# Two normalisations and the small operations of the softmax shifts on the Pool engine, and second scores one slot later over 128 rows

## What is computed

```python
x = x + tanh(g_xattn) * attention(layernorm(x), ctx, ctx, w_q, b_q, w_k, b_k, w_v, b_v, w_o, b_o)   # causal
x = x + tanh(g_ffn) * (mx_quantize(layernorm(x)) @ mx_quantize(weight).T + bias)
# layernorm(x) = (x - mean) / sqrt(var + 1e-5) over the width
# mx_quantize: blocks of 32 along the width, scale = max|block| / 7.5, then the nearest FP6 (E2M3) value
```

## Time and profile before

| what | value |
|---|---|
| median of 3 runs | 1609.66 us (1608.75 to 1612.53) |
| the profiled execution | 1625.08 us |
| its span | 1623.0 us |
| mean granted clock of PE in it | 0.955 of full speed |
| busy: PE, DVE, ACT, POOL | 89%, 76%, 65%, 36% of the span |

### The profile page before, as it was taken

The page is one execution under the profiler, slowest core; times in us unless marked ns, Lnnn a source line. Parts: engine busy times, 40 slices in busy tenths (PEclk is TensorE's granted clock), DMA queues, the critical chain, the costliest instruction groups (busy, mean ns, idle before and its releaser), DMA issues.

```text
span 1623.0 us, 34272 instructions
## 1 busy us (share of the span) xinstructions
PE 1448.8 (89%) x10333; PEld 1240.7 (76%) x10333; DVE 1233.2 (76%) x4731; ACT 1060.2 (65%) x3483; POOL 581.8 (36%) x881
## 2 busy tenths in 40 slices
PE   4788989999999998999998999999999999989976
PEld 4677777778878777877777878777787777778764
DVE  3677877878777788787787777777877778887863
ACT  2476667666666766766666666676666677766661
POOL 2223333443233343333333333344332344433343
PEclk9898999999999999999999999999999999999997
DMA  5244434343443443444444344344344344434420
GB/s 207 54 118 116 118 105 117 93 118 105 122 120 98 119 104 100 123 118 112 111 97 112 106 118 120 102 106 116 99 124 118 100 123 103 113 102 102 105 65 26
DMA packets 101807, 175.79 MB, mean 108 GB/s; under 512 B 14828, under 2 KB 18936, under 8 KB 101624
## 3 DMA queue, kind: packets, MB, share of 16 engines
q1 hardware_dynamic: 101624, 173.60, 41.3%
HBM read 56.11 MB, written 16.78 MB: 45 GB/s over the span
## 4 chain that ended last, share of the span: by engine, by line
DVE 42%; PE 29%; ACT 13%; issue 12%; DMA 2%; SPq 1%; POOL 0%; DVEq 0%; ACTq 0%
DVE all_probs L784 8%; PE proj L472 7%; DVE stack L820 7%; ACT all_probs L637 6%; PE proj L474 6%; PE proj L473 6%; DVE qk L841 4%; PE oT_ps L543 3%; DVE xs L897 3%; PE proj L565 3%; DVE stats L825 3%; DVE oT_lo L867 2%; DVE x L849 2%; DVE shift_rows L811 2%; DMA stack<-qk 2%
## 5 line engine op out<-in xcount | busy, mean ns | idle before, releaser
L637 ACT ACTIVATE all_probs<-all_probs,neg_max 128x128 f32<-128x128 f32 (+1 forms) x1024 | 457.8, 451 | 320.1 <-DVE neg_max L784 313.5
L784 DVE CUSTOM_DVE_ANT_0 all_probs<-s_ps,causal 128x128 f32<-128x128 f32 (+1 forms) x1024 | 322.4, 351 | 241.5 <-PE s_ps L515 226.3
L408 POOL TENSOR_SCALAR_AFFINE_SELECT all_probs<-all_probs 128x256 f32<-128x256 f32 x512 | 209.1, 409 | 777.4 <-ACT all_probs L656 777.4
L656 ACT ACTIVATE all_probs<-sT_ps 128x384 f32<-128x384 f32 x512 | 250.1, 489 | 139.3 <-PE sT_ps L528 138.1
L527 PE MATMUL sT_ps<-stack 104*128 104x256 f32 x512 | 178.0, 348 | 28.5 <-DVE stack L820 27.5
L637 ACT ACTIVATION_READ_ACCUMULATOR all_probs<-all_probs,neg_max 128x1 f32 x1024 | 196.3, 192 | 0.0
L472 PE MATMUL proj<-cT_hi,wk_hi 128*128 128x256 f32 x512 | 155.6, 304 | 29.0 <-DVE cT_lo L861 29.0
L514 PE MATMUL s_ps<-stack 96*128 96x256 f32 x512 | 155.7, 304 | 24.0 <-DMA stack<-qk 19.1
L820 DVE CAST stack<-shift_rows 8x256 fp32r<-8x256 f32 x512 | 159.5, 312 | 10.2 <-DVE shift_rows L811 0.6
L472 PE MATMUL proj<-aT_hi,wq_hi 128*128 128x256 f32 x512 | 152.2, 297 | 4.5 <-DVE aT_lo L861 4.5
L473 PE MATMUL proj<-cT_lo,wk_hi 128*128 128x256 f32 x512 | 146.2, 286 | 0.0
(11 more groups left out here) (133 smaller groups left out, 3918.2 us busy)
## 6 DMA issues: line engine op xcount, KB each, us to landing
stack<-qk SPq DMA_DIRECT2D x768, 128.0 KB, 2.4
cs<-in_ctx SPq DMA_DIRECT2D x32, 512.0 KB, 3.7
xs<-in_x SPq DMA_DIRECT2D x32, 512.0 KB, 4.5
x<-in_x SPq DMA_DIRECT2D x32, 512.0 KB, 3.9
out<-x SPq DMA_DIRECT2D x32, 512.0 KB, 3.1
vs<-in_L_xattn_w_k SPq DMA_DIRECT2D x2, 512.0 KB, 5.1
all_probs<-in_L_xattn_w_q SPq DMA_DIRECT2D x2, 512.0 KB, 6.4
all_probs<-in_L_xattn_w_v SPq DMA_DIRECT2D x2, 512.0 KB, 10.4
```

The costliest lines, as they stand in the source:

```text
L408: nc.gpsimd.affine_select(out=p, in_=p, compare_op=ALU.is_ge, fill=no, base=0, pattern=[[0, 2], [1, P]], channel_multiplier=-1).then_inc(t ...
L637: last = nc.scalar.activation(probs[:, n % P_RING, cols], probs[:, n % P_RING, cols], ACT.Exp, scale=-1.0, bias=neg_max[:, G % R_RING, t, ...
L656: nc.scalar.activation(probsT[:, n % PT_RING, :], sT_ps[n % 2][:, 0:3 * P], ACT.Exp, scale=-1.0).then_inc(pT_ok, 1)
L784: last = nc.vector.tensor_tensor_reduce(probs[:, n % P_RING, cols], s_ps[n % 2][:, cols], causal[:, (1 - t) * P:], 1.0, MASKED, ALU.add, A ...
```

## The change

- `shifts` is divided. POOL now computes ln(den) - neg_max twice (unrounded, and rounded as the high part), their difference `rest`, and near_one * den. DVE only adds near_one - 1 to `rest` as the low part, transposes and copies as before. The high part no longer holds the correction.
- `normalise` and `normalise_x` run on POOL: `normalise` one slot earlier in the program's order (2 slots behind `o`, ahead of `scaled`), `normalise_x` behind the power in slot 10, ahead of that slot's `shifts`.
- `T_LAG` is 7 and `AV_LAG` 16. With them values are weighed in slots 6 and 14 and split in 7 and 15, and `SLOT_PARTS` moves the light slots along.
- `stack` has 128 rows; rows 104 to 127 are set to zero at the start, and the second scores run over 128 rows.

```diff
-T_LAG = 6
-AV_LAG = 15
+T_LAG = 7
+AV_LAG = 16
-SLOT_PARTS = (3, 3, 3, 3, 3, 1, 3, 3, 3, 4, 3, 3, 3, 1, 4, 3)
+SLOT_PARTS = (3, 3, 3, 3, 3, 3, 1, 3, 3, 4, 3, 3, 3, 4, 1, 3)
...
-        stack = sb("stack", [ROWS + SHIFT, 2, 3 * PAIR, S], F32R)
+        stack = sb("stack", [P, 2, 3 * PAIR, S], F32R)
...
@@ gpsimd
+            nc.gpsimd.memset(stack[ROWS:, 1, :, :].bitcast(F32), 0.0).then_inc(zeros_ok, 1)
...
+            def shifts(G):
+                its = G % R_RING
+                pool.wait_ge(max_ok, GROUP * (G + 1))
+                pool.wait_ge(ln_ok, G + 1)
+                if G:
+                    pool.wait_ge(rows_ok, G)
+                nc.gpsimd.tensor_tensor(bare, ln_den[:, its], neg_max[:, its], ALU.subtract).then_inc(bare_ok, 1)
+                nc.gpsimd.tensor_tensor(shift_cols[:, :, 0:GROUP].bitcast(F32R), ln_den[:, its], neg_max[:, its],
+                                        ALU.subtract).then_inc(bare_ok, 1)
+                pool.wait_ge(bare_ok, 2 * G + 2)
+                nc.gpsimd.tensor_tensor(rest, bare, shift_cols[:, :, 0:GROUP], ALU.subtract).then_inc(r_ok, 1)
+                pool.wait_ge(exp_ok, G + 1)
+                nc.gpsimd.tensor_tensor(near_one[:, :, :], near_one[:, :, :], den[:, its], ALU.mult).then_inc(r_ok, 1)
+            def normalise(b, t):
+                pool.wait_ge(rs2, 2 * b + t + 1)
...
+                nc.gpsimd.tensor_scalar(yz[:, t, :], x1[:, b % 2, t, :], mom2[:, t, 0:1], var2[:, t:t + 1],
+                                        ALU.subtract, ALU.mult).then_inc(y_ok, 1)
+            def normalise_x(b):
+                pool.wait_ge(rs1, b + 1)
+                for t in range(T):
+                    nc.gpsimd.tensor_scalar(xs[:, b % 2, t, :], xs[:, b % 2, t, :], mom1[:, t, 0:1],
+                                            var1[:, t:t + 1], ALU.subtract, ALU.mult).then_inc(xn_ok, 1)
...
                         if i == 0:
                             choices()
-                    for ago, stage in ((1, deviation), (4, scaled), (6, dequantised), (8, with_bias)):
+                        normalise_x(i)
+                    if (G := shift_group(g)) is not None:
+                        shifts(G)
+                    for ago, stage in ((1, deviation), (2, normalise), (4, scaled), (6, dequantised), (8, with_bias)):
@@ scalar, logarithms
-                    act.wait_ge(r_ok, 2 * G)
+                    act.wait_ge(cols_ok, G)
@@ vector
+            nc.vector.memset(stack[ROWS:, 0, :, :].bitcast(F32), 0.0).then_inc(q_zeros_ok, 1)
...
             def shifts(G):
...
                 dve.wait_ge(r_ok, 2 * G + 2)
-                nc.vector.tensor_tensor(shift_cols[:, :, GROUP:SHIFT].bitcast(F32R), shift,
-                                        shift_cols[:, :, 0:GROUP], ALU.subtract).then_inc(cols_ok, 1)
+                nc.vector.scalar_tensor_tensor(shift_cols[:, :, GROUP:SHIFT].bitcast(F32R), near_one[:, :, :], -1.0,
+                                               rest, ALU.add, ALU.add).then_inc(cols_ok, 1)
```

More of the change, by code:

```diff
@@ L124, in fused_kernel @@
         bare = shift_cols[:, :, SHIFT:SHIFT + GROUP]
-        shift = shift_cols[:, :, SHIFT + GROUP:SHIFT + 2 * GROUP]
+        rest = shift_cols[:, :, SHIFT + GROUP:SHIFT + 2 * GROUP]
         oT_hi = sb("oT_hi", [P, KC, S], F32R)
@@ L166, in fused_kernel @@
         choice_ok = sem("choice_ok")
+        zeros_ok = sem("zeros_ok")
+        q_zeros_ok = sem("q_zeros_ok")
         bias_in = sem("bias_in")
@@ L391, in _ @@
                                         channel_multiplier=1).then_inc(chooser_ok, 1)
+            pool.wait_ge(ident_ok, 2)
+            pool.wait_ge(chooser_ok, 2)
+            nc.gpsimd.memset(stack[ROWS:, 1, :, :].bitcast(F32), 0.0).then_inc(zeros_ok, 1)
+            pool.wait_ge(zeros_ok, 1)
             def choices():
@@ L396, in choices @@
                 nc.gpsimd.tensor_copy(
-                    stack[ROWS:, 1, :, :].rearrange("c (n h) s -> c n h s", h=GROUP),
+                    stack[ROWS:ROWS + SHIFT, 1, :, :].rearrange("c (n h) s -> c n h s", h=GROUP),
                     chooser[ROWS:ROWS + SHIFT, :].unsqueeze(1).unsqueeze(3).to_broadcast(
@@ L813, in shifts @@
                 dve.wait_ge(rows_ok, G + 1)
-                if G >= 6:
+                if G == 0:
+                    dve.wait_ge(q_zeros_ok, 1)
+                elif G >= 6:
                     dve.wait_ge(sT_done, GROUP * (G - 5))
@@ L817, in shifts @@
                 for e in range(GROUP):
-                    to = stack[ROWS:, 0, at:at + GROUP, :].rearrange("c h (t e l) -> c h t e l", t=T, e=GROUP)[:, :, :, e]
+                    to = stack[ROWS:ROWS + SHIFT, 0, at:at + GROUP, :].rearrange("c h (t e l) -> c h t e l", t=T, e=GROUP)[:, :, :, e]
                     rows = shift_rows[e * DK:e * DK + SHIFT, :, :].unsqueeze(1).to_broadcast([SHIFT, GROUP, T, DK])
@@ L869, in output_lo @@
                                         ALU.subtract).then_inc(olo_ok, 1)
[L871 to L878, removed]
             def block_maxima(b, t):
@@ L892, in scales @@
                 nc.vector.reciprocal(amax[:, own], amax[:, own]).then_inc(inv_ok, 1)
[L894 to L897, removed]
-                                            var1[:, t:t + 1], ALU.subtract, ALU.mult).then_inc(xn_ok, 1)
             def step(i):
@@ L906, in step @@
                         weight_lo(*chunk)
-                    for ago, stages in ((4, (scales,)), (3, (block_maxima,)), (2, (normalise,))):
+                    for ago, stages in ((4, (scales,)), (3, (block_maxima,))):
                         for _, _, kind, half, b in finished(g, ago):
@@ L926, in step @@
                         moments(i + 1, (0, 1), xs[:, i % 2], stats1, mom1, var1, st1, mo1, va1)
-                    if s == ln1_slot(i) + 1 and live(i):
-                        normalise_x(i)
             for i in range(STEPS):
```

17 lines of the change are left out of this document (4 added, 13 removed).

## The result

The changed kernel takes 1772.95 us (median of 4 runs, 1772.26 to 1775.22) against 1610.42 us (4 runs, 1608.75 to 1612.53) for the kernel before on the same chip: a ratio of 1.101, 95% interval 1.099 to 1.103. It is 10% slower, where 0.6% faster was forecast; 1773 us is also far outside the range of 1568 to 1640.

What follows compares the result with a forecast made beforehand. No engine full, PE nearest (89% busy), waiting mainly in slot 12 for DVE. 0.3 + 0.2 - 0.1 = 0.4 us a step, 13 us over 32 steps, less 3 at the end: 10 us, giving 1600 us; range 1568 to 1640.

Steps and rivals of the forecast that it cites:

- The place: PE's big wait in slot 12, 1.62 us, was traced back to DVE's work in slot 10, including its shifts.
- The small operations: Slot 10, four 8-element operations on POOL: 0.19 us each taken, 0.28 and 0.55 kept for the range.
- From DVE's maxima of slot 11 to PE: Slots 11 to 12: from the start of DVE's maxima to PE taken as 1.47 us, from the earlier trace.
- 128 rows at nothing: Second scores over 128 rows instead of 104: matmul time was not expected to depend on rows, cost nothing.
- The removed waits: Waits for `stack`, its DMAs and most for `cT_lo` disappear, but slot 12 waits that much longer; worth nothing by themselves.
- the first rival: POOL becomes the bound of slot 10: 35 us turn the gain into a loss, 1635 us, at dearest 1677; chance 0.27.
- a `tensor_scalar` of 128x512 on POOL: Two in slot 10 between the power and DVE's work: 0.63 us each, ends 0.41 and 1.12 us.
- the triangle: POOL's one-input operation in the trace: 409 ns for 256 elements, 188 for 4; its 0.88 ns an element priced `tensor_scalar`.
- DVE's one operation, the transpose and the casts take 1.70 us: Slot 10, after POOL's small operations: DVE's remaining part of the shifts, with its duration read from the earlier trace.
- a gain that might come when DVE is freed: Slot 10: DVE free and POOL quick bring slot 12 0.6 us earlier, 19 us, 1581, or 1565 with clock; chance 0.20.
- The clock, a rival of its own: Longer wait in slot 12 gives ten more steps a lower-clock spell, costing 16 us: no change, 1610 us; chance 0.13.
- the forecast of 1040 us: DVE's busy time in the profile after was to be near 1040 us, with 6.1 us a step taken from it.

Runs made afterwards that it cites:

- e4: Changed kernel with `stack` at 104 rows again and without its two memsets: 1773.83 us, 1.097 of the kernel before.
- e8: Kernel before with only T_LAG 7, AV_LAG 16 and the new SLOT_PARTS: 1612.61 us, 0.993 of the kernel before.
- e12: Changed kernel with other forms in place of POOL's `tensor_scalar`, normalisations left incomplete: one operation with a column 1.58 us; its time is no measure.
- e3: Changed kernel with both `normalise_x` and `normalise` back on DVE: 1663.97 us, 1.029 of the kernel before.
- e5: e3 with POOL's `with_bias` of half 1 and residual additions moved to later slots (12, 13, 15): 1577.73 us, 0.972 of the kernel before.
- e6: Changed kernel with POOL's `with_bias` of half 1 and residual additions moved to slots 12, 13, 15: 1735.3 us, 1.070 of the kernel before.
- e7: Kernel before with POOL's `with_bias` of half 1 and residual additions moved to slots 12, 13, 15: 1559.12 us, 0.961 of the kernel before.
- e1: Changed kernel with the shifts ahead of `normalise_x` on POOL in slot 10: 1571.39 us, 0.972 of the kernel before.
- e9: Kernel before with the edits of e7 and e8 together: 1548.3 us, 0.954 of the kernel before.

## Why the prediction was wrong

**Right.** The place, first of all: slot 12 and, behind it, DVE's shifts of slot 10; nearly every other wait of PE has gone, but for `cT_lo`. The small operations: 0.20 us measured, 0.19 taken. From DVE's maxima of slot 11 to PE, 1.47 us taken: 1018.43 - 1016.94 = 1.49. 128 rows at nothing (e4). The removed waits nearly worthless by themselves (e8: 0.7%). And the first rival names the half of the mechanism that is POOL's, as the new bound of slot 10. It gave this 0.27 and priced it at 35 us, 77 at the most. The other half, DVE's casts, stands in none of the rivals as a cost.

**The first step that failed** is the term "a `tensor_scalar` of 128x512 on POOL", 0.63 us with ends at 0.41 and 1.12 us. It measured 2.08. Two of them are 2.9 us a step dearer than the sum has them. The nearest row was taken to be the triangle, because it too has one tensor input, and the two-input row was taken as the ceiling. Neither is a bound: the triangle is another instruction (0.88 ns an element), and the number of tensor inputs didn't order the prices, as e12 shows. The prediction called 1.12 us, together with 0.55 for the small ones, improbable, from no row at all. Its support for the rival, that every two-input row of POOL is above 1 us, holds for the large ones only (the power is at 549 ns). The Trainium skill, GPSIMD Engine Reference, section Engine selection, says POOL is about half as fast as the Vector engine with two inputs and roughly at line rate with one; here the one-input form is the slow one, 2.08 us against 0.50 on DVE, and the measurement decides. Its warning against elementwise work on POOL pointed the right way, for another form and by too little.

**The second step that failed** is "DVE's one operation, the transpose and the casts take 1.70 us", read from the earlier trace rows. In the changed kernel L834 starts at 1013.34 and the maxima at 1016.94, 3.60 us. The 1.70 were measured at a place where POOL, done with the power at 1026.10, sat idle beside the casts. The prediction moved the casts to the moment when POOL starts its additions of slot 11 and kept their old price. The sign was in its own rows and was used for the wrong operation: `normalise_x` at 1156 ns against 509 for the same shape was put into a rival as a gain that might come when DVE is freed. What had to be asked was which of DVE's operations would stand beside POOL's additions next. e3, e5, e6 and e7 show it.

**The sum again.** 2 x (2.08 - 0.63) + (3.60 - 1.70) = 4.8 us a step. The forecast had a step shorter by 0.4 us; it became longer by 4.3, a difference of 4.7. So these two terms hold the miss, 150 us of the 157 by which the profiled execution (1772.26) missed the 1615 us forecast for it. The clock, a rival of its own at 16 us, adds nothing to it that these numbers show. The mean granted clock fell from 0.955 to 0.908, and the transposes behind the longer idle piece take 1.11 us instead of 0.66, but PE's busy time is the same, 1447.3 against 1448.8 us. A part of the time at the lower clock falls where PE waits anyway: in the step shown the granted clock is 1.00 from 1011.2 to 1015.5 us and 0.50 from 1015.6 to 1018.4, with PE idle throughout. What the lower clock costs the changed kernel shows only against e1, 33 us of busy time; what made up for that against the kernel before was not taken apart.

**Why nothing of the gain was left.** DVE did lose work: by its lines 104 us of normalisations, and the five small operations of the shifts went from 112 to 26.5 us. The casts took back 52 (159.5 to 211.8 us) and the memset 5. Its busy time fell by only 92, where these lines would make 133: in part because the small operations had overlapped one another and the lines count such time twice, which the forecast of 1040 us did too. But DVE then sat idle 6.25 us a step in the one place that counts. e1 shows what the change is worth when POOL's long operations stand behind the shifts: 2.8%. That is more than the 0.6% forecast, and no proof of it: the forecast had the long operations ahead of the shifts. e7 and e9 show that the larger part is to be had without moving anything from DVE to POOL.

**The range.** It ended at 1640 because it took in POOL's prices only up to 1.0 us. A price for which no row of the same form exists was bounded by rows of other forms and then narrowed twice, by choosing the middle and by calling the end improbable. With the ends of both, 1.12 and 0.55 us, the sum still gave only 1677. The chances don't follow from their own parts either: four fifths of 0.40, all of 0.20 and a third of 0.13 are 0.56 for faster, not 0.50.

## What to carry to other kernels

An operation moved to an engine on which the trace has no row of its form has no upper bound from other forms; give the slower case the weight of that ignorance, and place such an operation behind whatever another engine waits for, since the order alone was worth some 200 us here. When an operation is moved in time, ask what the neighbour engine does at its new place: here four casts or two `tensor_scalar`s of DVE took two to three times as long beside POOL's two-input additions (2.92 and 3.16 us against 1.19, 1.97 against 1.00), and a duration read where POOL is idle doesn't travel.

## What the runs showed of the hardware

POOL's `tensor_scalar` is dearer than its `tensor_tensor`: 2.08 us with two operations and columns, 1.93 with constants, 1.58 with one operation, against 1.06 with two tensor inputs, all for 128x512.

One by one, the casts of the changed kernel show how DVE is held up. These are three of the four of slot 10, from narrow windows of DVE's timeline:

```profile
1014.00 1.05 DVE L850 CAST stack<-shift_rows 8x256 fp32r<-8x256 f32 x1
...
1015.06 1.25 DVE L850 CAST stack<-shift_rows 8x256 fp32r<-8x256 f32 x1
...
1016.62 0.29 DVE L850 CAST stack<-shift_rows 8x256 fp32r<-8x256 f32 x1
```

The first ends at 1015.05, 0.16 us behind POOL's L468 (1013.63 to 1014.89); the second at 1016.31, 0.15 us behind L473 (1014.85 to 1016.16); undisturbed ones take 0.29. So here a cast that meets a running POOL operation of this kind is not slowed by a factor but held until that operation is over.

The same shows in e3 and in the kernel before. In e3 the first cast starts 0.07 us ahead of POOL's L453 (998.62 to 999.98) and takes its 0.29 us; the second meets it and ends 0.15 us behind it. In the kernel before it is the second `normalise_x` of slot 10 that is held, by L431. First two lines of e3, then two of the kernel before:

```profile
998.55 0.29 DVE L834 CAST stack<-shift_rows 8x256 fp32r<-8x256 f32 x1
998.85 1.28 DVE L834 CAST stack<-shift_rows 8x256 fp32r<-8x256 f32 x1
```
```profile
1027.46 1.48 POOL L431 TENSOR_TENSOR x<-x,add_f 128x512 f32<-128x512 f32 x1
1027.72 1.51 DVE L897 TENSOR_SCALAR xs<-xs,mom,var 128x512 f32<-128x512 f32 x1
```

The Trainium skill, SBUF — State Buffer, section Who interferes with whom, describes just this: copies and casts of DVE in its two-port modes share a port pair with POOL, whoever is first has it for its whole instruction, and the other blocks. The trace agrees with that rule for POOL's `tensor_tensor`; in which mode the casts ran, no row shows. Beside POOL's `tensor_scalar` of 2.1 us in e1 it doesn't: the four casts there took 1.71 us in all, 0.5 more than undisturbed. Why the one form blocks and the other hardly does, no run here shows.
